# Squares of every second tile's q and k made by GpSimd instead of ScalarE, and VectorE's round in another order

## The reference

```python
x = layernorm(x + attn(x))        # 16 heads of 64, own layer norm, q and k normalised to length 1
x = layernorm(x + xattn(x, ctx))  # 16 heads of 8, against 64 context tokens
x = layernorm(x + ffn(x))         # (x W1 + b1) W2 + b2, no function between
```

```python
xn = layernorm(x) * gamma
q, k, v = xn @ w_q, ...                       # 1024 wide each, 16 heads x 64
q = q / max(norm(q), 1e-12) * q_scale         # per token and head
k = k / max(norm(k), 1e-12) * k_scale
sim = 8 * q @ k.T - slope[h] * |distance|     # causal mask, two null keys in front
out = softmax(sim) @ v
```

## Time and profile before

| | us |
|---|---|
| median of 3 runs | 915.85 (914.98 to 917.3) |
| the profiled execution | 922.4 |
| its span, first to last instruction | 920.6 |

### The profile page before, as it was taken

The page is one execution under the profiler, slowest core; times in us unless marked ns, Lnnn a source line. Parts: engine busy times, 40 slices in busy tenths (PEclk is TensorE's granted clock), DMA queues, the critical chain, the costliest instruction groups (busy, mean ns, idle before and its releaser), DMA issues. The chain is left out here.

```text
span 920.6 us, 19543 instructions
## 1 busy us (share of the span) xinstructions
PE 804.6 (87%) x6469; PEld 582.9 (63%) x6469; DVE 716.6 (78%) x2504; ACT 663.2 (72%) x1994; POOL 424.2 (46%) x356
## 2 busy tenths in 40 slices
PE   5879989898998989898998989898998989888953
PEld 3657657575666757576675757566675757566622
DVE  6574686988879797888969797888969787887644
ACT  4386777959687786968777786968778695857521
POOL 0317063463717365472727356371836447273511
PEclk9599999999999999999999999999999999999965
DMA  6000001000100001000100001000100000000000
GB/s 204 11 6 2 12 2 36 7 2 11 31 12 7 13 7 36 1 6 14 30 13 7 13 7 31 6 7 13 27 16 7 7 7 25 7 7 7 7 1 12
DMA packets 26418, 15.62 MB, mean 17 GB/s; under 512 B 4304, under 2 KB 25552, under 8 KB 26320
## 3 DMA queue, kind: packets, MB, share of 16 engines
q1 hardware_dynamic: 26320, 14.38, 5.5%
HBM read 12.27 MB, written 2.10 MB: 16 GB/s over the span
## 5 line engine op out<-in xcount | busy, mean ns | idle before, releaser
L1578 POOL TENSOR_TENSOR pr<-pr,rden 128x512 f32<-128x512 f32 x192 | 192.9, 1039 | 170.3 <-DVE rden L1045 170.3
L1350 ACT ACTIVATE pr<-pr,nmin 128x256 f32<-128x256 f32 (+1 forms) x512 | 225.4, 447 | 0.0
L1030 DVE CUSTOM_DVE_ANT_0 pr<-psS,alibi,nullmin 128x256 f32<-128x256 f32 (+1 forms) x512 | 180.3, 413 | 16.9 <-PE psS L555 16.8
L577 PE MATMUL psT<-ident,pr 128*128 128x128 f32 x768 | 123.4, 287 | 18.5 <-POOL pr L1578 18.5
L555 PE MATMUL psS<-kT,qT 64*128 64x256 f32 (+1 forms) x1024 | 111.2, 345 | 32.1 <-DVE nmin L1030 30.4
L1569 POOL TENSOR_TENSOR qk<-qk,rn 128x1024 f32<-128x1024 f32 x64 | 121.0, 1910 | 32.7 <-DVE rn L883 32.7
L577 PEld LDWEIGHTS psT<-ident,pr 128*128 128x128 f32 x768 | 81.5, 142 | 54.9 <-POOL pr L1578 26.7
L555 PEld LDWEIGHTS psS<-kT,qT 64*128 64x128 f32 x1024 | 78.6, 188 | 58.6 <-issue 56.6
L1308 ACT ACTIVATE qk<-psJ 128x512 f32<-128x512 f32 x128 | 75.4, 591 | 47.4 <-PE psJ L445 47.1
L1350 ACT ACTIVATION_READ_ACCUMULATOR pr<-pr,nmin 128x1 f32 x512 | 99.0, 193 | 0.0
L986 DVE TENSOR_REDUCE ssq<-sq 128x16 f32<-128x1024 f32 x64 | 77.6, 1213 | 26.3 <-ACT sq L1316 26.3
(11 more groups left out here) (147 smaller groups left out, 1691.9 us busy)
## 6 DMA issues: line engine op xcount, KB each, us to landing
w1s<-w1b SPq DMA_DIRECT2D x8, 258.0 KB, 2.9
xres<-x SPq DMA_DIRECT2D x16, 128.0 KB, 2.1
w2s<-w2T SPq DMA_DIRECT2D x8, 256.0 KB, 3.2
out<-x SPq DMA_DIRECT2D x16, 128.0 KB, 1.8
xin<-x SPq DMA_DIRECT2D x15, 128.0 KB, 2.3
pr<-w_kv SPq DMA_DIRECT2D x2, 512.0 KB, 5.1
pr<-w_q SPq DMA_DIRECT2D x1, 512.0 KB, 3.6
wo<-wout SPq DMA_DIRECT2D x1, 512.0 KB, 7.7
```

The lines of the kernel that those rows point to most:

```text
L577: mm = pe.transpose(psT[c % 2][:, P * j:P * (j + 1)], pr[t][:, h, P * kt:P * (kt + 1)], ident[:])
L1030: dve.tensor_tensor_reduce(pr[t][:, h, :], psS[score_bank(t, c)][:, keys * j:keys * (j + 1)], alibi[:, h, SEQ - keys:SEQ], 1.0, nullmin[:, ...
L1350: act.activation(pr[t][:, h, :], pr[t][:, h, :], ACT.Exp, bias=nmin[:, t, h:h + 1], scale=-1.0, accum_out=dparts[:, t, h, 0:1]).then_inc(e ...
L1578: pool.tensor_tensor(pr[t][:, hs, :], pr[t][:, hs, :], rden[:, t, hs].unsqueeze(2).broadcast_to([P, heads, P * (t + 1)]), ALU.mult).then_i ...
```

## The change

The squares of tile 0 stay on ScalarE (`square_qk(n, half)`). Those of tile 1 are products of qk with itself on GpSimd, two of 128 x 1024, behind `x1_plus_bias` and ahead of `x2_plus_bias` in each iteration, one iteration later than ScalarE made them; in the prologue they stand ahead of the first `norm_qk`. They have a semaphore of their own. On VectorE the end of the third layer norm goes behind all of tile 0's masks, the sums of tile 1's squares move from ahead of tile 1's masks (first half) and behind its second chunk (second half) to behind the second and the third chunk, and the denominators of tile 0 come ahead of them.

```diff
             def sum_squares(n, t, half):
-                dve.wait_ge(qk_squared, 2 * (NT * n + t) + half + 1)
+                dve.wait_ge(qk_squared if t == 0 else qk_squared_pool, 2 * n + half + 1)
...
                 need(dve, probsT_ready, PC * (i - 1) + TILE_PC[0])
-                mask_scores(i, 0, (0, 1))
+                mask_scores(i, 0, (0, 1, 2, 3))
+                null_shift(i, 0)
                 if e:
                     ln3_end(i - 2)
-                mask_scores(i, 0, (2, 3))
-                null_shift(i, 0)
-                if p:
-                    sum_squares(i + 1, 1, 0)
                 need(dve, probsT_ready, PC * i)
                 for k in range(8):
                     mask_scores(i, 1, (k,))
                     if k == 1:
+                        denominators(i, 0)
                         if p:
-                            sum_squares(i + 1, 1, 1)
-                            floor_squares(1)
-                        denominators(i, 0)
+                            sum_squares(i + 1, 1, 0)
+                    if k == 2 and p:
+                        sum_squares(i + 1, 1, 1)
+                        floor_squares(1)
...
                 if f:
                     copy_qk(i + 2, 7)
-                    square_qk(i + 2, 1, 0)
-                    square_qk(i + 2, 1, 1)
                     copy_nullraw(i + 2)
...
+            def square_qk(n, half):
+                pool.wait_ge(qk_copied_act, chunks_to(QK_ACT, n, 4 + 2 * half + 1))
+                if half == 0:
+                    pool.wait_ge(ssq_ready, NT * n + 1)
+                v = qk[n % 2][1][:, HD * half:HD * (half + 1)]
+                pool.tensor_tensor(sq[:, HD * half:HD * (half + 1)], v, v, ALU.mult).then_inc(qk_squared_pool, 1)
...
+            square_qk(0, 0)
+            square_qk(0, 1)
             norm_qk(0, 0)
             norm_qk(0, 1)
...
                 if c:
                     x1_plus_bias(i - 1)
+                if p:
+                    square_qk(i + 1, 0)
+                    square_qk(i + 1, 1)
                 if e:
                     x2_plus_bias(i - 2, (i - 2) // 2)
                 norm_probs(i, 0)
```

More of the change, by code:

```diff
@@ L330, in program @@
         qk_normed = sem("qk_normed")
+        qk_squared_pool = sem("qk_squared_pool")
         probs_normed = sem("probs_normed")
@@ L1308, in copy_qk @@
                 act.activation(qk[n % 2][t][:, 512 * j:512 * (j + 1)], psJ[c % 2][:], ACT.Copy).then_inc(qk_copied_act, 1)
-            def square_qk(n, t, half):
-                act.wait_ge(qk_copied_act, chunks_to(QK_ACT, n, 4 * t + 2 * half + 1))
-                act.wait_ge(qk_copied_dve, chunks_to(QK_DVE, n, 4 * t + 2 * half + 1))
+            def square_qk(n, half):
+                act.wait_ge(qk_copied_act, chunks_to(QK_ACT, n, 2 * half + 1))
                 if half == 0:
-                    need(act, ssq_ready, NT * n + t)
+                    need(act, ssq_ready, NT * n)
                 col = slice(HD * half, HD * (half + 1))
-                act.activation(sq[:, col], qk[n % 2][t][:, col], ACT.Square).then_inc(qk_squared, 1)
+                act.activation(sq[:, col], qk[n % 2][0][:, col], ACT.Square).then_inc(qk_squared, 1)
             def qk_seed(n, t):
@@ L1416, in _ @@
             null_keys_seed()
-            square_qk(0, 0, 0)
+            square_qk(0, 0)
             copy_qk(0, 6)
             ln_seed("ln1", (0, 1), 2)
-            square_qk(0, 0, 1)
+            square_qk(0, 1)
             copy_qk(0, 7)
@@ L1423, in _ @@
             qk_seed(0, 0)
-            square_qk(0, 1, 0)
             for c in range(4):
                 copy_qk(1, c)
-            square_qk(0, 1, 1)
             qk_seed(0, 1)
@@ L1431, in _ @@
             copy_qk(1, 5)
-            square_qk(1, 0, 0)
+            square_qk(1, 0)
             copy_qk(1, 6)
             copy_qk(1, 7)
-            square_qk(1, 0, 1)
+            square_qk(1, 1)
             copy_v(0, 0)
@@ L1444, in _ @@
                     copy_v(0, 2 + k)
-            square_qk(1, 1, 0)
-            square_qk(1, 1, 1)
             copy_nullraw(1)
@@ L1506, in iteration @@
                     copy_qk(i + 2, 2)
-                    square_qk(i + 2, 0, 0)
+                    square_qk(i + 2, 0)
                 copy_aoT(i, 1, 0)
@@ L1515, in iteration @@
                     copy_qk(i + 2, 3)
-                    square_qk(i + 2, 0, 1)
+                    square_qk(i + 2, 1)
                 copy_pT(i, 11)
```

## The result

The changed kernel takes 1028.45 us (median of four runs, 1026.46 to 1029.42), the kernel before 916.58 us in the same comparison (914.98 to 921.27). The ratio is 1.119, with a 95% interval of 1.115 to 1.123: slower by 112 us. The forecast was 988 us with a range up to 1008. The sign held, and so did the mechanism up to TensorE's weighing; the size did not.

The account below looks back on a forecast made before the run. ScalarE's unbroken chain was taken to set a round's first half. 13 rounds of 4.97 us (64.6) plus 1.5, 2.0 and 4.5 made 72.6; on the profiled 922.4 that is 995, 6.5 lower as median: 988 us, range 940 to 1008.

Parts of the forecast that it names:

- Part 1: Round's end: without tile 1's squares on ScalarE, null copy and TensorE's value projection come earlier; gain 0.29 us a round.
- Part 2: VectorE, first half: denominators 0.79 us earlier, sums and everything after 1.67 late; net +1.45 us a round.
- Part 3: GpSimd's squares, 1.90 us each, are hidden but make VectorE wait; with three places, weighing +4.97 us a round.
- (a): Layer norm's variance, 0.07 us behind the first square's start, waits for it; first mask +1.37 us, denominators 0.53 later.
- (b): Floor of the sums, behind the denominators, waits for GpSimd's fourth normalising piece, started 0.21 us ahead; takes about 1.0.
- (c): add_h2's variance waits for GpSimd's second q and k piece, about 1.7 us; pT copy at 547.05 against 541.88.
- the clock: TensorE idling ahead of the weighing may halve its clock; up to 1.4 us a round, 19 us, 1007; not summed.
- The start: Before the repeating rounds, VectorE's waits add 1.5 us in the prologue, 2.0 in round 0, 4.5 in round 1.
- R1: (a) misses since VectorE's variance gets in first; +3.68 us a round, 972 us; chance 0.20.
- R2: (c) misses, variance gets in ahead of GpSimd's second piece; +3.1 us a round, 962 us; chance 0.14.
- R3: GpSimd doesn't block at these places, only VectorE's waits are left; 1.45 us a round, 940 us; chance 0.09.
- R4: Not slower: the pT copy doesn't decide, only 0.29 us a round from the null copy stays; 912 us; chance 0.11.

Follow-up runs that it names:

- e1: Against the kernel before: tile 1's squares on GpSimd, VectorE's order as before; 944.2 us, ratio 1.027.
- e10: As e1, with variance and floor as reductions over one element, without the 1e-5 and 1e-24; 934.1 us, ratio 1.018.
- e8: Against the kernel before: ScalarE's copy of the raw null scores put between its two tile-1 squares instead of behind both; 915.3 us, ratio 0.9970.
- e4: Against the changed kernel: variance and floor as reductions over one element, without the 1e-5 and 1e-24; 962.8 us, ratio 1.047.
- e11: As e4, with 13 filler transposes on TensorE a round, only ahead of turn_nulls, from round 2 on; 950.7 us, ratio 1.035.
- e2: Against the kernel before: only tile 0's denominators put ahead of tile 1's sums, squares all on ScalarE; 999.8 us, ratio 1.087.
- e6: Against the changed kernel: GpSimd's squares and its products of qk with rn in pieces of 512 elements instead of 1024; 1004.4 us, ratio 1.092.
- e7: Against the changed kernel: GpSimd's two squares put behind x2_plus_bias instead of ahead of it; 1029.2 us, ratio 1.119.
- e5: Against the changed kernel: 38 filler transposes a round in TensorE's two waits, nothing computed changes; 996.7 us, ratio 1.085.
- e3: Against the kernel before: only the third layer norm's end moved behind tile 0's masks; 921.7 us, ratio 1.003.
- e9: Changed kernel with both e4's one-element reductions and e5's 38 filler transposes; 977.2 us, ratio 1.064.

## Why the prediction was right or wrong

**What bounds the kernel: right.** Only the first half of a round had room, and all that changed in the repeating rounds is there.

**Part 1, squares off ScalarE: the gain is not shown.** With the squares of tile 1 gone from ScalarE no kernel was faster (e1 944, e10 934). e8 reaches the same wait by another way and brings 0.17 us a round, not 0.29.

**Part 2, denominators ahead of the sums: right.** +1.45 a round was the forecast with no wait for GpSimd, and e4 and e11 measure +1.50.

**Part 3, squares on GpSimd: right in each place, and booked under the wrong part.** A square takes 1.89 us (1.90 taken). The variance 1.84 (1.9), the floor 0.89 (about 1.0), the second variance 1.66 (about 1.7), the idle time before the denominators 0.99 in most rounds (0.87 in the one shown). That one is shorter than the 1.2 of Part 2, since the masks too are late by (a). The weighing is +4.73 for +4.97. But only (a) comes from the squares: e2 has (b) and (c) with all squares on ScalarE, and costs 80 us, where e1, with the squares and the old order, costs 24. Most of the change's price comes with VectorE's order, through the waits that this order brings.

The Trainium skill (SBUF — State Buffer, Who interferes with whom) tells of an exclusive lock on ports that the two engines share. e6 agrees: the wait halves with the length of GpSimd's instruction, 1.84 to 0.99 us. The same section says that a tensor_reduce "never contends" on trn2, and e4 agrees (0.15 us beside a running square). It also names instructions with two SBUF inputs, which e7's pnn and e10's L880 bear out (1.28 and 1.03 us).

**The failed step: the clock, named and left out of the sum.** The prediction said "I don't put it in the sum, since half of such a stretch would lie in the wait", and sized it at up to 1.4 us a round. It is 2.4: 7.2 at the join less the weighing's 4.8 (the mean of rounds 3 to 14), and e5 takes it away (31.8 us). The stretch is not 3.5 us long, as in round 0 of the kernel before, but 6.8 us in nearly every round, from 607.3 to 614.1 in the round shown, of which 2.1 lie in the second wait and 4.7 in work. The scores alone lose 0.94 us. The case had TensorE's two waits of 2.34 and 2.03 us in its own working ("now idles some 4.8 of 5 us") and the earlier trace rows as an instance of what follows such idling. It should have been the main case, with the waits' price and the clock's in one sum. Such a stretch isn't certain from the wait alone: the 1.70 us wait early in the round was followed by one in two rounds of the twelve.

**The start: the second mis-sized term.** Prologue, round 0 and round 1 were set at 1.5, 2.0 and 4.5. The first scores come 2.3 us later than before. Round 0's join is +3.5. Round 1's own scores and join are another 2.8 and 4.5 late, so 7.3. Together 13 us for 8. The waits were as foreseen. Those on rn, at the start of round 1, here with the two squares beside them and the scores that wait for them:

```profile
111.58 3.79 POOL L1572 TENSOR_TENSOR sq<-qk 128x1024 f32<-128x1024 f32 x2
```

```profile
111.70 1.82 DVE L882 SCALAR_TENSOR_TENSOR newt<-newt,ssq 128x32 f32<-128x32 f32 x1
113.55 1.86 DVE L884 SCALAR_TENSOR_TENSOR rn<-newt,seedq 128x32 f32<-128x32 f32 x1
```

```profile
116.27 2.08 PE L556 MATMUL psS<-kT,qT 64*128 64x128 f32 x16 [2.67 <-DVE qT L1021]
```

and the stretch at the end of the prologue (columns as above):

```profile
54.40:61.20 6.80, 6.80 (x40) 5.79 (x40) 3.95 (x24) 1.64 (x4) 0.00 (x0) 0.50 0.07 20
```

TensorE's wait of 2.67 us (2.6 forecast) is followed by 16 scores of 128 columns in 2.08 us, which take 1.16 in the rounds, so half clock again, and the 6.8 us from 54.40 on, with the first scores of round 0 in them, are at 0.50 throughout, where the kernel before was at 1.00 to 67.6. Part of this is shown by an execution that happened not to have the stretch at 54.40: in e5's, whose prologue is the same program, the clock is at 1.00 there, the first scores come at 55.51 instead of 56.78 and the first mask 1.31 behind them instead of 2.26. That is 2.2 of the 5 us. That the clock is the rest as well is argued from the rows; no run removed it there. e5's filler didn't: it made round 1 longer (weighing at 21.46 for 18.81).

**The sum.** Against the profiled executions the change costs 1029.4 - 922.4 = 107 us. The forecast had 72.6. Rounds 2 to 14 cost 92 us for 64.6: 13 x 2.4 = 31 for the clock, less 13 x 0.25 = 3 by which the weighing's delay was overestimated (round 2, counted among the 13, has no place (a), and its weighing is only 3.6 later). The start is 5 over, and the part behind the last round's scores 1.5. The rest of the 40 us between 988 and 1028 is the step from the profiled execution to the median: 6.5 us were taken off, as for the kernel before, and the kernel after lies only 1.0 below its own. The traces hint at why. In e2 and e3, whose prologue is that of the kernel before, TensorE's clock is full again from about 35 us on and the first scores come at 48.7, against about 44 us and 54.5 in the profiled execution of the kernel before; none of the nine traces with squares on GpSimd has its first scores ahead of 53.7. That the faster executions of the kernel before are those with the short prologue is likely and not shown.

**The rivals.** R1 (place (a) misses) and R2 (place (c) misses) fell: both waits are in every round from 3 to 14. The margins of 0.07 and 0.27 us came out as 0.08 and 0.26; that the first held on the side of the forecast was in part luck. R3 (only VectorE's waits are left) is what e11 makes of the change, at 951 us for 940. R4 (the late copy of pT doesn't decide) fell: the weighing follows that copy by 0.82 us.

**Slips in the working that decided nothing.** Rounds don't recur every 51.65 us: they take 51.65 and 53.1 us in turn, so the stretch to 578.7 leaves out the last 1.5 us of the round shown. R2's sum, 13 x 3.1 + 8, is 48 us and 964, not 46 and 962, and R1's 3.68 is 4.97 - 1.32 = 3.65.

## What to carry to other kernels

When an engine that sets nothing gets new work, don't ask whether it has the time; lay its new intervals over each small SBUF instruction of its neighbour, and expect that a collision which is pushed away can turn up at the next one (e7, e10). The same goes for a new order on the neighbour with no new work anywhere: that was 80 of the 112 us (e2). When a change makes TensorE wait in a stretch where it was busy, put the half clock behind the wait into the sum from the start: here it was 31 of 112 us, and the next rounds paid it again each time. The cheap tests are to give the idle TensorE exactly as much idle work as its wait holds (e11 gained by it, e9 lost by too much) and to swap single instructions for a form that doesn't collide, which prices the waits apart from the order.

## What the runs showed of the hardware

- A GpSimd product of a 128x1024 tile with itself takes 1.894 us, the same as one of two operands of which one is spread (1.913); GpSimd gains nothing from reading one tensor twice. In four pieces of 512 the same two squares take 4.03 instead of 3.75 us.
- VectorE's tensor_scalar, tensor_tensor and scalar_tensor_tensor on as little as 128x2 and 128x32 elements wait for the end of a GpSimd instruction that started ahead of them: from 0.15 to 0.2 us up to 1.03, 1.28, 1.66, 1.84 and 1.86. Reductions over one element (0.15, 0.19), masks out of PSUM (0.34 beside a square) and batch statistics (0.49 for two beside a product of q and k) don't.
- The profile counts such a wait as busy time. VectorE's sum rose from 716.6 to 775.4 us with the same instructions, and only a comparison of the durations of single rows tells it from work.
- Two waits of TensorE of 2.34 and 2.03 us, with 0.27 us of work between them, went with a granted clock of 0.5 for 6.8 us, which began between the two. With e4's two waits of 1.67 and 0.57 us it was 3.4 us in every second round. With fillers in the waits the clock stayed at 1.00 behind them from round 2 to 14 (e5, e9, e11). A wait of 1.70 us behind a stretch of work was followed by 3.4 us of half clock in two rounds of twelve and by none in the others.
